# A new order of calls on all queues, and 32 unread products ahead of TensorE's first transposes

## What is computed

```python
def fake_quant(x, s, z):
    q = clip(round(x / s + z), 0, 255)
    return (q - z) * s

x = x + tanh(g_xattn) * matmul(fake_quant(layernorm(x)), fake_quant(ctx))
n = layernorm(x)
logits = n @ route_w.T                    # 8 experts
best, e = top_k(logits, 1)
h = n @ A[e].T                            # rank 16
x = x + tanh(g_ffn) * best * (h @ Bw[e].T)
```

## Time and profile before

| what | us |
|---|---|
| median of 3 runs | 364.46 (363.89 to 364.64) |
| profiled execution, its own time | 363.53 |
| its span, first to last instruction | 361.7 |
| PE / DVE / ACT / POOL busy in it | 333.0 / 260.6 / 197.4 / 172.3 |
| moved by DMA | 87.63 MB, 242 GB/s over the span |

### The profile page before, as it was taken

The page is one execution under the profiler, slowest core; times in us unless marked ns, Lnnn a source line. Parts: engine busy times, 40 slices in busy tenths (PEclk is TensorE's granted clock), DMA queues, the critical chain, the costliest instruction groups (busy, mean ns, idle before and its releaser), DMA issues.

```text
span 361.7 us, 5854 instructions
## 1 busy us (share of the span) xinstructions
PE 333.0 (92%) x2237; PEld 186.4 (52%) x2262; DVE 260.6 (72%) x553; ACT 197.4 (55%) x129; POOL 172.3 (48%) x199
## 2 busy tenths in 40 slices
PE   0389999999999999999998999999999999999983
PEld 0244454546756466455464546464464555465751
DVE  3855799898967896958658587945588567585853
ACT  1888489778967262747999270524062413204460
POOL 2559267431265162545999056627064441605281
PEclk9999999999999999999999999999999999999999
DMA  7999999895769998899799996666939890443956
GB/s 301 400 387 404 366 387 380 289 348 173 284 182 212 289 251 291 270 266 294 176 366 157 262 320 121 181 111 177 212 138 158 225 288 31 93 84 59 304 220 232
DMA packets 93906, 87.63 MB, mean 242 GB/s; under 512 B 71844, under 2 KB 72868, under 8 KB 89764
## 3 DMA queue, kind: packets, MB, share of 16 engines
q1 hardware_dynamic: 93856, 87.11, 79.5%
q10 hardware_dynamic: 12, 0.00, 0.0%
HBM read 52.49 MB, written 16.78 MB: 191 GB/s over the span
## 4 chain that ended last, share of the span: by engine, by line
PE 77%; DVE 8%; DMA 7%; issue 2%; ACT 2%; POOL 2%; ACTq 0%; SPq 0%; DVEq 0%
PE main L1575 46%; DMA xs<-in_x 4%; PE hp L1613 4%; PE hp L1617 4%; PE hp L1614 4%; PE outp L1575 4%; PE outp L1658 4%; PE outp L1660 3%; PE outp L1659 3%; DVE bn L971 3%; PE turn L1609 2%; DMA prow<-in_g_ffn 2%; DMA out<-xs 1%; ACT x L753 1%; PE turn L1503 1%
## 5 line engine op out<-in xcount | busy, mean ns | idle before, releaser
L1575 PE MATMUL main<-q,qa 128*128 128x512 bf16 x841 | 194.6, 380 | 5.0 <-POOL q L593 2.3
L1575 PEld LDWEIGHTS main<-q,qa 128*128 128x128 bf16 x864 | 83.2, 98 | 101.2 <-issue 2.7
L586 POOL TENSOR_TENSOR yn<-y,yn 128x2048 f16<-128x2048 f32 x13 | 53.0, 4077 | 31.7 <-ACT y L788 31.7
L735 ACT ACTIVATE c<-stage,zpc,inv 128x2048 int8<-128x2048 f32 x24 | 49.9, 2086 | 7.7 <-DMA stage<-in_ctx 4.0
L593 POOL CAST q<-c 128x2048 bf16<-128x2048 int8 x24 | 45.1, 1893 | 15.3 <-ACT c L735 14.8
L782 ACT ACTIVATE yn<-xs,sc 128x2048 f16<-128x2048 f32 x11 | 23.0, 2093 | 53.4 <-POOL sc L579 49.6
L1104 DVE SCALAR_TENSOR_TENSOR xs<-main,cc,xs 128x512 f32<-128x512 f32 x45 | 33.3, 740 | 21.7 <-PE main L1575 21.5
L574 POOL TENSOR_SCALAR ve<-mv 128x1 f32<-128x1 f32 x16 | 3.1, 191 | 84.8 <-DVE mv L1137 81.8
L1184 DVE SCALAR_TENSOR_TENSOR xs<-outp,tsc,xs 128x512 f32<-128x512 f32 x44 | 31.2, 735 | 13.6 <-PE outp L1660 13.5
L971 DVE BATCH_NORM_STATS2 bn<-xs 128x6 f32<-128x512 f32 x52 | 32.1, 680 | 10.6 <-DMA xs<-in_x 10.6
L753 ACT ACTIVATE x<-xs,sc 128x2048 int8<-128x2048 f32 x12 | 25.0, 2087 | 24.5 <-POOL sc L566 24.4
(11 more groups left out here) (132 smaller groups left out, 435.2 us busy)
## 6 DMA issues: line engine op xcount, KB each, us to landing
stage<-in_ctx SPq DMA_DIRECT2D x24, 1024.0 KB, 7.9
xs<-in_x SPq DMA_DIRECT2D x13, 1024.0 KB, 6.5
out<-xs SPq DMA_DIRECT2D x12, 1024.0 KB, 5.0
yT<-in_ctx SPq DMA_DIRECT2D x4, 1024.0 KB, 9.2
y<-in_ctx SPq DMA_DIRECT2D x4, 1024.0 KB, 10.1
c<-in_x SPq DMA_DIRECT2D x3, 1024.0 KB, 7.4
out<-c SPq DMA_DIRECT2D x3, 1024.0 KB, 7.3
c<-in_L_ffn_A SPq DMA_DIRECT2D x1, 1024.0 KB, 11.5
```

The source lines that it names most:

```text
L586: pool.tensor_tensor(yn[:, 1, :], y[:, :], yn[:, 0, :], ALU.subtract).then_inc(s_ylo_made, 1)
L735: act.activation(c8_of(piece), place(piece), ACT.Identity, bias=zpc[:, 1:2], scale=inv[:, 1:2])\
L1575: last = pe.matmul(bank_of(n)[:, :], q1T(t)[:, k, :], q2[:, nb, k, :], start=(k == 0), stop=(k == KC - 1))
```

## The change

One helper for banks: the last two transposes of y of tile 15 go to the two main banks in place of turn[0] and turn[1], and wait for the last add_main instead of for low_part. One new helper, warm: products of a constant tile of ones into wp, read by nobody; it is called twice with 16 ahead of turn_q1(0, 0). Everything else is order: calls of all five lists change places, none is dropped or added. The diff has 1,259 lines; here is its core.

```diff
+        def y_bank(t, g):
+            return mainp[3 - g] if t == T - 1 and g >= 2 else turn[g % 2]
...
@@ SP
             load_x(0)
             load_x(1)
+            load_x(2)
             load_ctx(0)
             load_ctx(1)
-            load_x(2)
             load_ctx(2)
+            load_x(3)
             load_ctx(3)
+            load_a()
             load_ctx(4)
             load_ctx(5)
+            load_router()
             load_ctx(6)
             load_ctx(7)
-            load_x(3)
-            load_a()
-            load_router()
             load_ctx(8)
-            load_x(4)
             load_ctx(9)
...
             load_ctx(30)
+            load_ctx(31)
             load_x(9)
-            load_ctx(31)
...
@@ ACT, the start
             affine_first(1)
+            affine_x(1)
             affine_ctx(0)
-            affine_x(1)
+            affine_x(2)
             affine_ctx(1)
             affine_ctx(2)
-            affine_x(2)
             affine_ctx(3)
+            affine_x(3)
...
@@ ACT, the end
-            take_wh(14)
-            high_part(15, 2)
+            scale_part(14, 0)
             high_part(15, 3)
-            scale_part(14, 0)
             scale_part(14, 1)
...
@@ DVE, the start
             widen_first(1)
+            see_q1(0)
+            stats1(2)
+            widen_x(1)
             take_q1T(0, 0)
             take_q1T(0, 1)
-            see_q1(0)
-            widen_x(1)
             see_q1(1)
-            stats1(2)
             take_q1T(1, 0)
             take_q1T(1, 1)
             widen_x(2)
+            stats1(3)
             take_q1T(2, 0)
...
@@ DVE, tile 8
             add_experts(5, 0)
+            add_experts(5, 1)
             stats1(9)
             tile_terms(8)
             add_main(8, 0)
             add_main(8, 1)
-            add_experts(5, 1)
             add_experts(5, 2)
...
             add_main(9, 1)
             stats1(11)
-            add_experts(6, 2)
+            stats1(12)
             add_experts(6, 3)
+            add_experts(7, 0)
             add_main(9, 2)
...
+            add_experts(7, 2)
+            add_experts(7, 3)
+            stats1(13)
             add_main(10, 2)
...
@@ PE
+            def warm(n):
+                for k in range(n):
+                    pe.matmul(wp[:, 0:P], onesb[:, :], onesb[:, :], start=True, stop=True)
...
                 if g < 2:
                     wait_turn("y", t, g)
+                elif t < T - 1:
+                    pe.wait_ge(s_y_split, 4 * YT.index(t) + g - 1)
                 else:
-                    pe.wait_ge(s_y_split, 4 * YT.index(t) + g - 1)
+                    pe.wait_ge(s_half_added, 1)
+                    pe.wait_ge(s_main_added, UNIT[T - 1, NB - 1] + 1)
...
+            warm(16)
+            warm(16)
             turn_q1(0, 0)
             turn_q1(0, 1)
-            main(0, 0, 0)
             turn_q1(1, 0)
             turn_q1(1, 1)
-            main(0, 0, 1)
+            main(0, 0, 0)
             main(1, 0, 0)
-            main(1, 0, 1)
-            main(0, 0, 2)
-            main(1, 0, 2)
             turn_q1(2, 0)
             turn_q1(2, 1)
+            main(0, 0, 1)
+            main(1, 0, 1)
...
             main(3, 1, 3)
-            turn_a(2)
+            turn_a(3)
             column_sums(0, [2])
             main(0, 2, 0)
...
             main(0, 3, 1)
+            turn_b(0)
+            turn_b(1)
+            main(0, 3, 2)
             turn_b(2)
-            turn_b(3)
-            main(0, 3, 2)
             main(0, 3, 3)
             column_sums(1, [3])
             main(1, 3, 0)
+            turn_b(3)
             main(1, 3, 1)
             main(1, 3, 2)
             main(1, 3, 3)
+            turn_q1(4, 0)
+            turn_q1(4, 1)
             column_sums(2, [3])
...
             main(7, 2, 0)
+            main(7, 3, 0)
+            main(7, 2, 1)
             expert_product(4, 2)
-            main(7, 2, 1)
-            main(7, 3, 0)
+            expert_product(4, 3)
             main(7, 3, 1)
-            expert_product(4, 3)
-            turn_wh(5)
             main(7, 2, 2)
...
             main(8, 0, 2)
+            main(8, 1, 2)
+            expert_product(5, 2)
             main(8, 0, 3)
-            main(8, 1, 2)
             main(8, 1, 3)
+            expert_product(5, 3)
+            turn_wh(6)
             main(8, 2, 0)
...
             h_group(15, 1)
-            turn_y(15, 3)
             expert_product(14, 0)
             expert_product(14, 1)
+            expert_product(14, 2)
             h_group(15, 2)
             h_group(15, 3)
-            expert_product(14, 2)
             expert_product(14, 3)
```

More of the change, by code:

```diff
@@ L446, in _ @@
             load_ctx(12)
+            load_x(4)
             load_ctx(13)
@@ L471, in _ @@
             store(2)
+            load_ctx(25)
             load_ctx(26)
@@ L497, in _ @@
             flip_q1(10)
+            store(6)
             flip_high(9)
-            store(6)
+            load_x(13)
             flip_low(9)
             flip_q1(11)
-            store(7)
             flip_high(10)
@@ L505, in _ @@
             flip_q1(12)
-            load_x(13)
+            store(7)
+            store(8)
             load_x(14)
+            load_x(15)
             flip_high(11)
@@ L1289, in _ @@
             unit_terms(1, 3)
+            take_b(3)
+            scale_b()
+            take_q1T(4, 0)
+            take_q1T(4, 1)
             add_main(1, 3)
@@ L1319, in _ @@
             add_main(4, 1)
+            add_main(4, 2)
             gate(2)
-            take_q1T(5, 0)
-            add_main(4, 2)
+            add_experts(1, 0)
+            add_experts(1, 1)
             add_main(4, 3)
@@ L1325, in _ @@
             tile_terms(5)
-            add_experts(1, 0)
-            add_experts(1, 1)
+            add_experts(1, 2)
+            take_q1T(5, 0)
             take_q1T(5, 1)
-            add_experts(1, 2)
             add_experts(1, 3)
@@ L1430, in _ @@
             add_experts(9, 3)
+            stats1(15)
             tile_terms(13)
+            add_main(13, 0)
             gate(11)
+            add_main(13, 1)
             add_experts(10, 0)
-            add_main(13, 0)
-            add_main(13, 1)
-            stats1(15)
             add_experts(10, 1)
-            add_experts(10, 2)
             add_main(13, 2)
@@ L1441, in _ @@
             stats2_sum(13)
+            add_experts(10, 2)
+            add_experts(10, 3)
+            gate(12)
             tile_terms(14)
-            gate(12)
-            add_main(14, 0)
-            add_main(14, 1)
-            add_experts(10, 3)
             add_experts(11, 0)
@@ L1449, in _ @@
             add_experts(11, 2)
-            add_experts(11, 3)
+            add_main(14, 0)
+            add_main(14, 1)
             add_main(14, 2)
+            gate(13)
             add_main(14, 3)
-            gate(13)
             stats2_sum(14)
             tile_terms(15)
+            add_main(15, 0)
+            add_experts(11, 3)
             add_experts(12, 0)
-            add_main(15, 0)
             add_main(15, 1)
@@ L1681, in _ @@
             main(1, 0, 3)
+            turn_q1(3, 0)
             column_sums(2, [0])
             main(2, 0, 3)
+            turn_q1(3, 1)
             main(1, 1, 0)
+            main(0, 1, 0)
+            main(3, 0, 0)
+            main(3, 0, 1)
             main(1, 1, 1)
@@ L1697, in _ @@
             column_sums(2, [1])
+            main(3, 0, 2)
             main(2, 1, 3)
-            turn_q1(3, 0)
-            turn_q1(3, 1)
-            turn_a(0)
-            main(3, 0, 0)
             main(3, 1, 0)
@@ L1753, in _ @@
             main(2, 3, 2)
-            spread_scales()
-            turn_q1(4, 0)
-            turn_q1(4, 1)
+            main(2, 3, 3)
             turn_y(0, 0)
             turn_y(0, 1)
-            main(2, 3, 3)
-            h_group(0, 0)
+            spread_scales()
             column_sums(3, [3])
+            main(3, 3, 0)
+            main(3, 3, 1)
             turn_y(0, 2)
             turn_y(0, 3)
-            main(3, 3, 0)
-            main(3, 3, 1)
+            h_group(0, 0)
             main(3, 3, 2)
@@ L1768, in _ @@
             h_group(0, 1)
-            turn_y(1, 0)
-            turn_y(1, 1)
-            h_group(0, 2)
-            h_group(0, 3)
             column_sums(4, range(NB))
@@ L1855, in _ @@
             main(6, 3, 0)
+            main(6, 2, 2)
             main(6, 3, 1)
-            main(6, 2, 2)
+            main(6, 3, 2)
             main(6, 2, 3)
-            main(6, 3, 2)
             main(6, 3, 3)
+            h_rows_high(5)
             turn_q1(7, 0)
-            turn_q1(7, 1)
-            h_rows_high(5)
             expert_product(4, 0)
```

363 lines of the change are left out of this document (177 added, 186 removed).

## The result

| | before | after |
|---|---|---|
| median of 3 runs, us | 364.46 (363.89 to 364.64) | 366.91 (366.74 to 367.23) |
| profiled execution, us | 363.53 | 367.23 |
| its span, us | 361.7 | 365.4 |
| mean granted clock of TensorE | 1.000 | 0.985 |

The changed kernel is slower: ratio 1.0086, 95% interval 1.0068 to 1.0105. The forecast was 362.9, in a range of 361.0 to 365.0.

A forecast was written before the change was run, and what follows sets the result against it. PE's queue was taken to set the end. From 363.53 us profiled, less 2.1 of lead, plus 0.1 at the 192 wait and 0.5 at the end: 362.0; the median stands 0.93 above, so 362.9, range 361.0 to 365.0.

The forecast's parts named there:

- the lead at tile 6: PE's gain over the old order by the end of tile 5, summed from the opening on: 2.1 us.
- What bounds the kernel: PE, busy 333.0 of 361.7 us: its queue sets the end.
- The opening: Start to main(0, 2, 0): products start 4.4 us later, no stand at 43 to 46, 0.2 us gained.
- The row of the end: Trace of before, 358 to 360 us: PEclk 1.00 after PE stands, taken to show a 3.2 us stretch leaves the clock up.
- The clock rival: Opening: the clock falls in PE's 3.4 us idle stretch or isn't raised; +1.0 and +0.9 or more, 364.3 us; chance 0.20.
- 71 to 86 us: Calls of main between the turn_b: PE meets no wait, ends spread_scales at 83.9 against 85.7; lead 1.9 us.
- 86 to tile 5: Calls, DVE, ACT and flips' waits followed: gaps left under 0.4 us, lead comes to 2.1 us.
- From tile 6 on: Only loads followed, not every call; new PE gaps in 140 to 190 or 195 to 336 named as a sign of error.
- The wait at 192: main(8, 2, 0), with x9 behind load_ctx(31): chain 18.2 us against PE's work 16.7, wait 1.5 us against 1.42.
- The slower rival: load_ctx(31) and flip_q1(9) hold x9 and x10 longer than PE's added work covers; 2.7 us more, 365.6 us; chance 0.13.
- The end: Tile 15: expert_product(14, 2) earlier costs 0.65, scale_part(14, 0) wait 0.3, turns save 0.4; 0.5 us later, between 0 and 0.9.
- The 32 products: From about 10.3 to 13.7 us, ahead of the first transposes: cost nothing and raise the clock, which stays up.

The follow-up runs named there:

- e3: The changed kernel with 48 more unread products between turn_q1(0, 1) and turn_q1(1, 0); 365.09 us, ratio 1.0030.
- e12: The mended kernel: changed kernel with 48 opening products, load_x(9) before load_ctx(31), expert_product(14, 2) and scale_part(14, 0) moved back, 20 products before turn_wh(15); 362.88 us.
- e11: Every list is the kernel before's up to tile 5 and the changed kernel's from there on; 368.88 us, ratio 1.0139.
- e2: The kernel before with the 32 unread products alone added; 365.13 us, ratio 1.0027.
- e13: The mended kernel without the 48 unread products ahead of turn_q1(1, 0); 366.29 us, ratio 1.0072.
- e6: The changed kernel with load_x(9) back ahead of load_ctx(31); 366.67 us, ratio 1.0085.
- e4: The changed kernel with 28 unread products between expert_product(14, 3) and turn_wh(15); 366.85 us, ratio 1.0079.

## Why the prediction was wrong

By the profiled executions the forecast was 1.5 us less than before (362.0) and the change brought 3.7 more, a miss of 5.2. It has three parts: the lead at tile 6 was 0.6 us and not 2.1 (1.5), the stretch from there to main(9, 0, 1) lost 2.6 and not 0.1 (2.5), and the end 1.7 and not 0.5 (1.2).

**What bounds the kernel.** Right: PE's queue set the end in every run.

**The opening.** The sum gave main(0, 2, 0) at 54.4, so main(0, 2, 3) at 57.0; it came at 58.0. Two terms failed. POOL's small steps, priced 2.0 us from the old order, took 2.6, since the new one puts VectorE's widening beside them, and that made piece 1 0.8 later: with the clock up, too, main(0, 2, 3) starts at 57.4 (e3) or 57.8 (e12). And the clock fell at 19.6: 0.3 to 0.6. The row of the end, PEclk 1.00 at 358 to 360, was not the precedent I took it for: there PE had worked for over 300 us at the upper level ahead of its 3.2 us, here for 6 us. That the longer work is what kept it up isn't shown either: at the end of after it fell (357.5) with as much work behind it. The clock rival's mechanism came true; for the opening itself its price of 1.0 was too high, as the pieces would have held PE anyway. The Trainium skill's rule ("TensorE: Matmul & The Clock Gate", Part 4: PE-mode transpose), by which transposes don't count as work, would also give a fall here; no run here parts the transposes from the idle 3.2 us beside them, so it is neither shown nor refuted.

**71 to 86 us.** Right: 1.7 us gained between main(0, 2, 3) and main(3, 3, 0) (before adds 2.1 of lag, after 0.4), with no wait, as summed.

**86 to tile 5.** The lead stayed but for 0.2 (0.85 at h_rows_low(2), behind a DMA of 6.0 us, less 0.7 that before lost in small waits).

**From tile 6 on: the step that decided.** I followed only the loads here, took nothing lost outside the wait at 192, and warned of new gaps in 140 to 190 and 195 to 336. They are there: 0.5, 0.9 and 0.6 us at four products, each from the order of a list (VectorE: statistics ahead of an addition, a gate ahead of two; TensorE: turn_wh(5) directly ahead of expert_product(5, 0)); e11 shows that this stretch loses as much with the opening of before. With main(9, 0, 0)'s 0.85 the stretch lost 2.6 us more than before, against my 0.1.

**The wait at 192.** x9's load grew by 2.7, the end of my 1.6 to 2.7 that I didn't take; it landed 14.9 us after expert_product(4, 3), and the forecast said 14.6. The wait was 1.1, forecast 1.5. Right in size, wrong in worth: I judged the load by that wait alone ("the next one ... nothing"), but the same late x9 also sets flip_q1(9). Undone in the mended kernel it gives 2.2 us. The slower rival had this place and cause right; its price of 2.7 is near the 2.2 of the mended kernel, but it isn't what made the change slow by itself, as the four waits ahead of it took 2.0.

**The end.** The summed terms were right: 0.65 for the three products (1.96 against 1.32), 0.3 for the wait for scale_part(14, 0) (0.4), less 0.4 for the turns (0.3). Missed: 0.95 at h_rows_low(14), and the clock's fall. The sum was 0.5, the trace 1.7 up to expert_product(15, 0); in the mended kernel the whole end comes to 0.7, not clear of noise.

**The 32 products.** They cost PE nothing, as forecast, but the clock they raised (at 16.2) fell again at 19.6: the change without them (e1) is no slower, and in the mended kernel their 0.6 us isn't clear of noise. That on the old order they cost 1.0 (e2) I hadn't expected.

**What stays open.** Why flip_low(2) takes 6.0 us in after, e2 and e13 and 4.3 in before, e1, e3 and e12, and so why 48 products at 16 us should spare a wait at 113 us; and where the executions of e13 above its lowest lose up to 4 us.

## What to carry to other kernels

An order is worth what its waits are on every engine: replay the calls of the engines that empty banks, not the loads alone, over the whole span, before a gain in one stage is booked. A load moved behind another delays every chain that starts from it, so price it at each reader, not at its first wait. And don't drop a mending because it shows nothing alone: x9's place was worth nothing measurable in e6 and 2.2 us beside the others, and the four mendings together gave 4.3 us where the best single one gave 2.0.

## What the runs showed of the hardware

- The granted clock fell at 19.6 us after PE had worked from 10.3 and stood from 16.2 to 19.5 (transposes 1.78 us in place of 1.06); with 48 products in the gap it stayed up. The column PEclk isn't enough to see this: in e1 it reads 1.00 in 14.5 to 27.8 while the durations are those of the lower level. The first clock record of that trace is at 27.55 (20.5 in before), and ahead of it the column has nothing to go by.
- A slow clock on the last products cost less than it stretched them: in after the last addition ends 5.2 us behind the start of expert_product(15, 0) and in before 4.0, but the spans end 8.3 and 8.2 us behind it (7.6 in e4). From the last addition to the end of the span it is 3.1 us in after, 3.6 in e4 and 4.2 in before. That the stores end sooner because the slow additions spread them out is a reading; no run tests it.
- DMA transposes into yT take 4.3 to 6.2 us to land in after and 4.3 to 7.8 in before. Before and after issue the one of flip_low(2) at nearly the same time (107.8 and 108.0) and see 4.3 and 6.0.
- A small step of GpSimd takes 1.07 us beside VectorE's int8 to bf16 widening and 0.23 alone (after, 17.73 and 28.21); another 1.36 and 0.33 (before, 13.61 and 9.88).
